# One projection per batch with its rounded halves stacked through DRAM, separate banks for the two score passes, and the value bias moved into the gelu

## The chip, the cores and the metric

The kernel runs on one core of a Trainium2 chip. The metric is the device time of one execution in microseconds (us). Every number of the profile comes from one profiled execution.

## The reference

Eight blocks follow each other on a residual x of 8 batches x 128 rows x 512 columns: four times an attention, then a feed-forward layer. The change touches the first attention alone:

```python
x = x + _L0_xattn_ref(_layernorm(x), ctx, mask, Wq, bq, Wk, bk, Wv, bv, Wo, bo)
# W = 128 (window), H = 8 heads, D = 128, DK = 64, dh = 8; patches are [d, 128] windows of a batch
q = einsum('ed,bdw->bew', Wq, qp) + bq[:, None]
k = einsum('ed,bdw->bew', Wk, qp) + bk[:, None]
val = einsum('ed,bdw->bew', Wv, vp) + bv[:, None]
scores = einsum('bhdi,bhdj->bhij', qh, kh) / sqrt(dh)
scores = where(mask > 0, scores, -1e9)
attn = softmax(scores)
o = gelu(einsum('bhij,bhdj->bhdi', attn, vh))
out = (einsum('de,bew->bdw', Wo, o) + bo[:, None]) * mask
```

## The kernel before

The order of every engine is written out by hand in `l0_attention`, and the engines meet only at semaphores. SP issues the DMAs of this stage.

The work is cut into 16 **units**: unit u is batch b = u // 2 and group g = u % 2 of four heads. The score products run in float32r, which keeps fewer bits than float32, so each head's eight rows of q and of k are split into a rounded part and a rest, and three products are stacked along the contraction: hi·hi, hi·lo, lo·hi. A head fills a slot of 32 partitions: three times eight rows, a row that carries the negated maximum (24) and a row for the mask (25). Before the change the stacking comes from the projection itself: `wq` and `wk` hold every head's weights three times, so that each unit needs two projections of 128x512 in float32 (`project`, L625 and L626), and selection columns (`C_SELQ`, `C_SELK`) pick the parts out on ScalarE and GpSimd.

A unit's steps, with the letters that the prediction uses:
- **P**: two projections into `K_BANK` and `Q_BANK`; ScalarE takes `q_lo` (L448) and `k_hi` (L456), VectorE makes `kf` (L514) and `q` (L521), GpSimd makes `k` (L432) and every batch's `key_mask` (L361, L364).
- **S**: plain scores, queries against keys, 16 matmuls for a unit in two halves (L655), each half into a pair of banks, `S_BANK + 2 * (s % 2)`.
- **M**: maximum over the keys on VectorE, one `tensor_reduce` for a half (L553).
- **T**: four transposes that turn the maxima (L664).
- **L**: `lower`, VectorE adds the turned maxima to `q` (L562).
- **K**: keyed scores, keys against queries, 16 matmuls (L672) in two halves, into the same pairs of banks as S.
- **E**: the exponential, one ScalarE activation for a half (L464).
- **V**: 16 float32 matmuls with the values (L683), which the trace shows as 32.
- **C**, **O**, **D**: ScalarE takes the sums out (L471), four transposes (L690), VectorE divides (L542, L544).
- **PV**: once per batch the values' projection (L633), which shares `K_BANK`; VectorE adds the bias bv (L531).

After the 16 units `turn_back`, a gelu, `project_out` and the residual follow for each of the 8 batches. Statistics of x (L100, L102) and `normalise` (L502) are VectorE's.

## Time and profile before

| | us |
|---|---|
| median of 3 runs | 1110.77 |
| lowest and highest | 1109.35, 1111.75 |
| span of the profiled execution, first to last instruction | 1113.1 |
| PE busy in the span | 956.4 (86%) |
| DVE, ACT, POOL busy | 710.9, 459.4, 368.4 |
| first attention: first keyed product to last division | 23.88 to 156.11 |

No time of the profiled execution beside its span is given; the span alone stands 2.3 us over the median of the runs. Busy time of PE is the union of its matmuls, which are pipelined and whose ends are modelled. In a timeline a row is a group of like instructions: start, duration, engine, line, operation, output and inputs, count, and in brackets the idle time of the engine before it with what ended it. PEclk is the granted TensorE clock, 1.00 for 2.4 GHz and 0.50 for 1.2 GHz; before 27 us it reads 1.00 although the matmuls there take as long as later ones at 0.50.

### The profile page before, as it was taken

To read this page: it belongs to the slowest core of one execution; us is meant where nothing else is said; L and a number is where in the kernel's file an instruction comes from. 1 tells how busy PE (TensorE), PEld (TensorE's weight loads), DVE (VectorE), ACT (ScalarE), POOL (GpSimd) and SP (SyncE) were. 2 spreads that over 40 slices of the span, in tenths; PEclk is the share of its full clock that TensorE was granted. 3 is DMA by queue.
4 is the path that set the end of the run, shared out by engine and by line. 5 is a ranking of instruction groups with operands and counts; after the bars stand their busy time and mean duration, and the time that the engine had idled before them with its cause. 6 is when DMAs were issued, how large, how long until landed. Compare 5 with 4: busy or idle time off the path is not lost. (4 is left out here: it accounts for less than half of the span.)

```text
span 1113.1 us, 14911 instructions
## 1 busy us (share of the span) xinstructions
PE 956.4 (86%) x4939; PEld 617.6 (55%) x4939; DVE 710.9 (64%) x1186; ACT 459.4 (41%) x672; POOL 368.4 (33%) x352
## 2 busy tenths in 40 slices
PE   5888884999999999999887688899987698779997
PEld 2555552655666666664454344444464465447886
DVE  5676547396778777874958853477745788445434
ACT  2454432324656566662225332344412465334130
POOL 5244203104757656752221320200010122038431
PEclk9899865899999999999987799699997899979999
DMA  8000102233978967655404100000003100022001
GB/s 315 1 2 1 57 2 90 87 133 129 335 278 306 348 240 262 221 190 199 160 1 180 39 0 1 20 2 1 1 1 132 67 1 0 1 94 77 24 15 39
DMA packets 32988, 112.69 MB, mean 101 GB/s; under 512 B 4304, under 2 KB 4624, under 8 KB 29840
## 3 DMA queue, kind: packets, MB, share of 16 engines
q1 hardware_dynamic: 25392, 87.08, 21.3%
q0 software_dynamic: 7520, 24.65, 6.4%
q8 instruction: 41, 0.67, 0.2%
q14 instruction: 35, 0.29, 0.1%
HBM read 132.69 MB, written 16.78 MB: 134 GB/s over the span
## 5 line engine op out<-in xcount | busy, mean ns | idle before, releaser
L1208 POOL DMA_INDIRECT f_picks<-f_turn_xn,f_target x47 | 114.1, 2428 | 75.1 <-ACT f_turn_xn L1097 74.5
L1624 PE MATMUL banks<-f_t_dn,f_z 128*128 128x512 f32 x188 | 88.5, 593 | 0.6 <-issue 0.6
L1352 DVE TENSOR_TENSOR f_gu_lo<-f_t_gu,f_gu_hi 128x2048 fp32r<-128x2048 f32 x24 | 55.0, 2293 | 14.2 <-ACT f_gu_hi L1083 11.5
L1352 DVE TENSOR_TENSOR f_xn_lo<-f_t_gu,f_xn_hi 128x2048 fp32r<-128x2048 f32 x23 | 52.7, 2292 | 16.4 <-ACT f_xn_hi L1083 16.4
L1202 POOL DMA_INDIRECT f_turn_xn<-f_xn_rows,f_token x47 | 47.4, 1008 | 43.0 <-DVE f_token L1346 18.7
L106 POOL TENSOR_TENSOR a_ahead_var_eps<-mean_var,eps 128x1 f32<-128x1 f32 x16 | 3.0, 190 | 162.5 <-DVE mean_var L102 162.5
L2315 ACT ACTIVATE a_e<-banks 128x1024 f32<-128x1024 f32 x32 | 32.8, 1024 | 53.3 <-PE banks L2414 53.2
L1090 ACT ACTIVATE f_sil<-banks 128x256 f32<-128x256 f32 x47 | 18.1, 384 | 79.3 <-PE banks L255 79.3
L164 PE MATMUL banks<-ident,f_turn_xn 128*128 128x128 f32 x96 | 22.0, 384 | 32.6 <-DVE f_turn_xn L172 32.6
L1083 ACT CAST f_gu_hi<-f_t_gu 128x2048 fp32r x24 | 45.7, 1905 | 9.5 <-DMA f_t_gu<-in_f_gu 7.2
L1083 ACT CAST f_xn_hi<-f_t_gu 128x2048 fp32r x23 | 43.7, 1901 | 12.9 <-DMA f_t_gu<-in_f_gu 10.5
L100 DVE BATCH_NORM_STATS2 stat<-x_res 128x6 f32<-128x512 f32 x64 | 44.3, 692 | 5.2 <-DMA x_res<-in_x 3.3
L464 ACT ACTIVATE a_e<-banks 128x1024 f32<-128x1024 f32 x32 | 31.0, 1021 | 36.6 <-PE banks L672 36.6
L432 POOL TENSOR_TENSOR a_k<-a_kf,a_k_sel 128x512 fp32r<-128x512 f32 x16 | 20.8, 1301 | 73.3 <-ACT a_k_sel L456 73.3
L1624 PEld LDWEIGHTS banks<-f_t_dn,f_z 128*128 128x128 f32 x188 | 32.1, 190 | 23.3 <-issue 23.2
L2352 DVE TENSOR_REDUCE a_mx<-banks 128x8 f32<-128x1024 f32 x32 | 39.1, 1222 | 8.5 <-PE banks L2396 8.5
L553 DVE TENSOR_REDUCE a_mx<-banks 128x8 f32<-128x1024 f32 x32 | 37.6, 1219 | 6.3 <-PE banks L655 6.3
L253 PE MATMUL banks<-f_gu_hi,f_xn_hi 128*128 128x512 f32 x96 | 40.0, 417 | 1.8 <-issue 1.7
L2428 PE MATMUL banks<-a_e,raw 128*32 128x512 f32 x128 | 35.4, 631 | 4.5 <-DVE a_ot_lo L2344 4.5
L106 POOL TENSOR_TENSOR f_ahead_var_eps<-mean_var,eps 128x1 f32<-128x1 f32 x24 | 9.0, 375 | 91.4 <-DVE mean_var L102 91.4
L253 PE MATMUL banks<-f_xn_hi 128*128 128x512 f32 x92 | 38.2, 415 | 1.1 <-issue 1.1
L3087 DVE TENSOR_TENSOR f_square<-f_relu 128x512 f32<-128x512 f32 x16 | 19.5, 1224 | 30.6 <-ACT f_relu L3030 25.6
(415 smaller groups left out, 2635.5 us busy)
## 6 DMA issues: line engine op xcount, KB each, us to landing
f_t_gu<-in_f_gu SPq DMA_DIRECT2D x47, 1024.0 KB
f_t_dn<-in_f_dn SPq DMA_DIRECT2D x47, 512.0 KB, 4.4
f_t_gu<-f_picks SPq DMA_DIRECT2D x8, 1024.0 KB, 5.1
f_xn_rows<-f_turn_xn SPq DMA_DIRECT2D x9, 256.0 KB, 2.6
x_res<-in_x SPq DMA_DIRECT2D x8, 256.0 KB, 6.9
a_ctx<-in_ctx SPq DMA_DIRECT2D x2, 1024.0 KB, 13.5
a_out_mask<-in_mask SPq DMA_DIRECT2D x1, 2048.0 KB, 15.8
a_ct<-in_ctx_turned SPq DMA_DIRECT2D x4, 512.0 KB, 7.9
```

Source lines behind the costliest of these rows:

```text
L100: dve.bn_stats(self.stat[:, b, :], src).then_inc(self.stat_ready, 1)
L253: pe.matmul(out, w_hi, m_hi, start=start, stop=False)
L464: act.activation(e[:, u % 2, 2 * (s % 2):2 * (s % 2) + 2, :], ps[:, s_banks(s), :], ACT.Exp, scale=scale).then_inc(exp_ready, 1)
L553: dve.tensor_reduce(mx[:, :, PAIR * (s % 2) + A0_MAX_ROW:PAIR * (s % 2 + 1):A0_SLOT].rearrange("p w r -> p r w"), ps[:, s_banks(s), :].rea ...
L1083: act.copy(t_gu_hi[t % 2], t_gu[:, bass.ds(i, 1), :, :].rearrange("p i c n -> p (i c n)"))\
L1202: pool.indirect_dma_start(t_rows[:, t % F0_BUFS, :], None, dram["f0_xn_rows"], bass.IndirectOffsetOnAxis(ap=token[:, t:t + 1], axis=0))\
L1208: pool.indirect_dma_start(dram["f0_picks_flat"], bass.IndirectOffsetOnAxis(ap=target[:, t:t + 1], axis=0), t_y[:, t % F0_BUFS, :], None).t ...
L1352: dve.tensor_tensor(t_gu_lo[t % 2], t_gu[:, bass.ds(i, 1), :, :].rearrange("p i c n -> p (i c n)"), t_gu_hi[t % 2].bitcast(F32), ALU.subtr ...
L1624: mm = pe.matmul(ps[:, TY_BANK + t % 2, :], t_zt[:, t % 2, c, :], t_dn[:, t % F0_BUFS, c, :], start=c == 0, stop=c == F0_IC - 1)
L2315: act.activation(e[:, u % 2, 2 * (s % 2):2 * (s % 2) + 2, :], ps[:, s_bank(s):s_bank(s) + 2, :], ACT.Exp, scale=scale).then_inc(exp_ready, 1)
L2352: dve.tensor_reduce(mx[:, tiles, A2_MAX_ROW:P:A2_SLOT].rearrange("p m r -> p r m"), ps[:, s_bank(s):s_bank(s) + 2, :].rearrange("p r (m j) ...
L2428: mm = pe.matmul(ps[A2_VSLOT * i:A2_VSLOT * (i + 1), O_BANK + u % 2, :], v[:, b // HB, b % HB, g * A2_PER_GROUP + i, :], e[:, u % 2, i, :] ...
```

## The change

- **One projection per batch.** q and k come out of one 128x512 projection (`wqk`, 64 rows of q above 64 of k). VectorE adds the bias and applies the mask (`keys_queries`), ScalarE rounds (`upper_part`), GpSimd subtracts (`lower_part`; for batch 0 VectorE).
- **Stacking by DMA.** SP writes the parts of a batch to a DRAM tensor `a0_parts` with five DMAs (`store`) and reads them back with four (`fetch`) into one of three buffers `a0_st`, 26 rows for each head. Constant rows and the mask row are written once, for all batches, by three more DMAs.
- **Three batches are projected ahead** (`A0_EARLY`); later ones follow in the odd units 1, 3, 5, 7 and 9.
- **Own banks.** S always writes banks 4 and 5, K always banks 6 and 7. A half of S therefore waits for the maximum of the half before, a half of K for the exponential before. PV has a bank of its own.
- **Loads.** Batches 3 to 7 of x are loaded after the fetches of batches 0, 1 and 2.
- **Moved to other engines.** `normalise` of batches 3 to 7 and one mask operation per batch are GpSimd's; the values are taken out by ScalarE without bias, and bv is the bias of the gelu.
- **Rows.** S and K contract over 26 rows instead of 32.

The core of the diff:

```diff
+                    def store(b):
+                        qs, ks = slice(0, A0_HEADS), slice(A0_HEADS, 2 * A0_HEADS)
+                        sp.wait_ge(qk_hi_ready, b + 1)
+                        hi, lo = qk_hi[:, b % 2, :].bitcast(F32), qk_lo[:, b % 2, :].bitcast(F32)
+                        sp.dma_start(part_of(b, slice(0, 2 * A0_HEADS), 0), hi).then_inc(parts_stored[b % 2], 16)
+                        sp.dma_start(part_of(b, qs, 1), hi[0:A0_DK]).then_inc(parts_stored[b % 2], 16)
+                        sp.dma_start(part_of(b, ks, 2), hi[A0_DK:P]).then_inc(parts_stored[b % 2], 16)
+                        sp.wait_ge(qk_lo_ready, b + 1)
+                        sp.dma_start(part_of(b, qs, 2), lo[0:A0_DK]).then_inc(parts_stored[b % 2], 16)
+                        sp.dma_start(part_of(b, ks, 1), lo[A0_DK:P]).then_inc(parts_stored[b % 2], 16)
+                    def fetch(b):
+                        sp.wait_ge(parts_stored[b % 2], 16 * A0_WRITES * (b // 2 + 1))
+                        if b < A0_BUFS:
+                            sp.wait_ge(st_zeroed, b + 1)
+                        else:
+                            sp.wait_ge(keyed_done, 2 * A0_GROUPS * (b - A0_BUFS + 1))
+                        for r in range(A0_PER_GROUP):
+                            sp.dma_start(st[r * A0_SLOT:r * A0_SLOT + A0_ROWS, b % A0_BUFS, :, :].bitcast(F32),
+                                         parts[b, r::A0_PER_GROUP].rearrange("j e n -> e j n")).then_inc(st_loaded[b % A0_BUFS][r // 2], 16)
...
+                    store(0)
+                    sp.wait_ge(fixed_stored, 16 * 3)
+                    fetch(0)
+                    load_x(3)
+                    store(1)
+                    fetch(1)
+                    load_x(4)
+                    load_x(5)
+                    store(2)
+                    fetch(2)
+                    load_x(6)
+                    load_x(7)
...
+                    kept(1)
+                    lower_part(1)
+                    clear(1)
+                    kept(2)
+                    lower_part(2)
+                    for i in range(2):
+                        pool.memset(v[:, i, :, :, :], 0.0).then_inc(zeroed, 1)
...
+                    clear(2)
+                    for b in range(3, B):
                         first.scale(pool, b)
+                        kept(b)
+                        normalise(b)
+                        lower_part(b)
...
+                    maximum(0)
+                    maximum(1)
+                    for b in range(A0_EARLY, B):
+                        statistics(b)
+                    for u in range(UNITS + 2):
+                        if u >= 2:
+                            divide(u - 2)
+                        if u + 1 < UNITS:
+                            maximum(2 * u + 2)
+                        if batch_at(u) is not None:
+                            keys_queries(batch_at(u))
                         if u < UNITS:
                             lower(u)
...
                         if u + 1 < UNITS:
                             maximum(2 * u + 3)
...
                     def scores(s):
...
+                        pe.wait_ge(st_loaded[b % A0_BUFS][s % 2], 16 * 2 * (b // A0_BUFS + 1))
+                        if s >= 1:
+                            pe.wait_ge(max_ready, s)
...
                     def keyed(s):
...
+                        if s >= 1:
+                            pe.wait_ge(exp_ready, s)
...
                     for u in range(UNITS + 1):
                         if u < UNITS:
-                            keyed(2 * u)
-                            keyed(2 * u + 1)
-                        if u == 0:
-                            project(2)
+                            turn_max(u)
+                        if u + 1 < UNITS:
+                            scores(2 * u + 2)
+                        if u >= 1:
+                            keyed(2 * u - 1)
+                        if batch_at(u) is not None:
+                            project(batch_at(u))
+                        if values_at(u) is not None:
+                            project_values(values_at(u))
                         if u >= 1:
                             values(u - 1)
...
                         if u + 1 < UNITS:
-                            scores(2 * u + 2)
                             scores(2 * u + 3)
+                        if u < UNITS:
+                            keyed(2 * u)
                         if u >= 1:
                             turn_outputs(u - 1)
-                        if u + 3 < UNITS:
-                            project(u + 3)
-                        if u + 1 < UNITS:
-                            turn_max(u + 1)
```

PE's order inside the loop. First before the change, an odd and an even unit (L672 is K, L683 V, L633 PV, L655 S, L690 O, L625 and L626 P, L664 T):

```order
L672 MATMUL banks<-a_q,a_k 128x128 x16
L683 MATMUL banks<-a_e,a_v 32x128 x16
L633 MATMUL banks<-raw,a_ctx 128x64 x4
L655 MATMUL banks<-a_k,a_q 128x128 x16
L690 MATMUL banks<-ident,a_osb 128x128 x4
L625 MATMUL banks<-a_xn,raw 128x512
L626 MATMUL banks<-a_xn,raw 128x512
L664 MATMUL banks<-ident,a_mx 128x128 x4
```

Then the change, from T of unit 3 to O of unit 2 (L735 is T, L726 S, L745 K, L697 P, L704 PV, L756 V, L763 O):

```order
L735 MATMUL banks<-ident,a_mx 128x128 x3
L726 MATMUL banks<-a_st 128x128 [waits a0_max_ready,a0_st_loaded_2_0]
L726 MATMUL banks<-a_st 128x128 x7
L745 MATMUL banks<-a_qm,a_st 128x128 [waits a0_exp_ready,a0_q_max_ready]
L745 MATMUL banks<-a_qm,a_st 128x128 x7
L697 MATMUL banks<-a_xn,raw 128x512 [waits a0_qk_ready,a0_xn_ready]
L704 MATMUL banks<-raw,a_ctx 128x64 [waits a0_v_ready,a0_ctx_loaded_1]
L704 MATMUL banks<-raw,a_ctx 128x64 x3
L756 MATMUL banks<-a_e,a_v 32x128 [waits a0_on_ready,a0_v_ready,a0_exp_ready]
L726 MATMUL banks<-a_st 128x128 [waits a0_max_ready,a0_st_loaded_2_1]
L745 MATMUL banks<-a_qm,a_st 128x128 [waits a0_exp_ready,a0_q_max_ready]
L763 MATMUL banks<-ident,a_osb 128x128 [waits a0_o_ready]
```

The two halves of S and of K no longer stand together: V and, in an odd unit, P and PV stand between them, and V waits for the second exponential of its own unit.

SP's queue in the change, from the write of batch 1 to the load of x for batches 6 and 7 (L418 to L423 are `store`, L432 is `fetch`, L394 `load_x`):

```order
L418 DMA a_parts<-a_qk_hi 16x8x512 [waits a0_qk_hi_ready]
L422 DMA a_parts<-a_qk_lo 8x8x512 [waits a0_qk_lo_ready]
L432 DMA a_st<-a_parts 26x4x512 [waits a0_st_zeroed,a0_parts_stored_1]
L432 DMA a_st<-a_parts 26x4x512 x3
L394 DMA x_res<-in_x 128x512 x2
L418 DMA a_parts<-a_qk_hi 16x8x512 [waits a0_qk_hi_ready]
L422 DMA a_parts<-a_qk_lo 8x8x512 [waits a0_qk_lo_ready]
L432 DMA a_st<-a_parts 26x4x512 [waits a0_st_zeroed,a0_parts_stored_0]
L432 DMA a_st<-a_parts 26x4x512 x3
L394 DMA x_res<-in_x 128x512 x2
```

Before, all eight loads of x were issued at the head of the queue with nothing that SP waited for between them; now the last two stand behind three waits for writes to land.

## Rows read from the trace of the kernel before

**Rows 1.** Windows: the loop, then two stretches of it at the low clock level

```profile
core 0: us, PE busy (x) PEld busy (x) DVE busy (x) ACT busy (x) POOL busy (x), PEclk, DMA share, GB/s
23.88:156.11 132.23, 110.81 (x1248) 75.78 (x1249) 79.65 (x122) 60.02 (x77) 42.04 (x33) 0.84 0.04 15
...
106.20:113.00 6.80, 6.31 (x20) 3.62 (x20) 3.77 (x7) 1.64 (x3) 1.27 (x1) 0.50 0.00 0
137.00:157.20 20.20, 15.40 (x169) 11.75 (x169) 5.29 (x10) 7.48 (x9) 0.00 (x0) 0.50 0.11 44
```

**Rows 2.** Timeline, an odd unit at the high level: start and duration first

```profile
67.19 0.69 PE L672 MATMUL banks<-a_q,a_k 32*128 32x128 f32 x16 [0.78 <-DVE a_q L562]
...
67.81 1.08 PE L683 MATMUL banks<-a_e,a_v 128*32 128x128 f32 x32
67.89 1.94 ACT L464 ACTIVATE a_e<-banks 128x1024 f32<-128x1024 f32 x2 [1.37 <-PE banks L672]
...
68.83 1.10 PE L633 MATMUL banks<-raw,a_ctx 128*128 128x64 f32 x8
...
69.86 0.78 PE L655 MATMUL banks<-a_k,a_q 32*128 32x128 f32 x16
...
70.56 2.36 DVE L553 TENSOR_REDUCE a_mx<-banks 128x8 f32<-128x1024 f32 x2 [0.17 <-PE banks L655]
...
71.06 1.02 PE L625 MATMUL banks<-a_xn,raw 128*128 128x512 f32 x2
...
71.92 1.02 PE L626 MATMUL banks<-a_xn,raw 128*128 128x512 f32 x2
...
72.97 0.42 PEld L664 LDWEIGHTS banks<-ident,a_mx 128*128 128x128 f32 x4 [0.86 <-DVE a_mx L553]
```

**Rows 3.** The page's costliest groups: the exponential of one half (E)

```profile
L464 ACT ACTIVATE a_e<-banks 128x1024 f32<-128x1024 f32 x32 | 31.0, 1021 | 36.6 <-PE banks L672 36.6
```

**Rows 4.** Timeline at the low level, and the loop's last division

```profile
125.26 1.91 PE L625 MATMUL banks<-a_xn,raw 128*128 128x512 f32 x2
...
126.96 1.92 PE L626 MATMUL banks<-a_xn,raw 128*128 128x512 f32 x2
...
137.74 1.14 PE L672 MATMUL banks<-a_q,a_k 32*128 32x128 f32 x16 [0.78 <-DVE a_q L562]
...
138.81 1.93 PE L683 MATMUL banks<-a_e,a_v 128*32 128x128 f32 x32
...
140.68 1.41 PE L655 MATMUL banks<-a_k,a_q 32*128 32x128 f32 x16
...
141.83 2.36 DVE L553 TENSOR_REDUCE a_mx<-banks 128x8 f32<-128x1024 f32 x2 [4.15 <-PE banks L655]
...
144.24 0.72 PEld L664 LDWEIGHTS banks<-ident,a_mx 128*128 128x128 f32 x4 [1.51 <-DVE a_mx L553]
...
155.82 0.29 DVE L544 TENSOR_TENSOR a_on_all<-banks,a_rec 128x128 f32<-128x128 f32 x1
```

**Rows 5.** Waits of the first 150 us: total, times and longest

```profile
PE banks L672 <- DVE a_q L562: 12.5, 16, 0.8
```

**Rows 6.** Timeline of the start of the kernel

```profile
0.95 1.84 POOL L405 MEMSET a_v<- 128x1024 f32 x2
1.20 0.42 SPq L378 DMA_DIRECT2D raw<-in_a_first  x1
...
5.83 2.05 PE L625 MATMUL banks<-a_xn,raw 128*128 128x512 f32 x2 [5.83 <-DVE a_xn L502]
...
12.33 1.26 POOL L432 TENSOR_TENSOR a_k<-a_kf,a_k_sel 128x512 fp32r<-128x512 f32 x1 [0.49 <-ACT a_k_sel L456]
...
19.19 2.01 POOL L361 TENSOR_SCALAR raw<-raw,a_cols 128x512 f32<-128x512 f32 x1
...
23.88 1.15 PE L672 MATMUL banks<-a_q,a_k 32*128 32x128 f32 x16 [0.78 <-DVE a_q L562]
```

**Rows 7.** Tile f_xn_rows: landing of nine writes of 256 KB to DRAM

```profile
DMA to landing us min/median/max: 2.0/3.9/9.2
```

More of the change, by code:

```diff
@@ new lines, in load_x, with load_ctx, load_mask @@
+                    def load_x(b):
+                        sp.dma_start(core.x[:, b, :], dram["x"][b]).then_inc(x_loaded[b], 16)
+                    def load_ctx(i):
+                        sp.dma_start(ctx[:, 2 * i:2 * i + 2, :], dram["ctx"][2 * i:2 * i + 2].rearrange("b p s -> p b s"))\
+                          .then_inc(ctx_loaded[i], 16)
+                    def load_mask(i, first, last):
+                        out = late_mask[:, :, :] if first >= HB else core.raw[:, 1, first * D:last * D]
+                        src = dram["mask"][first:last]
+                        if first < HB:
+                            src = src.rearrange("b s -> (b s)")
+                        sp.dma_start(out, src.partition_broadcast(P)).then_inc(mask_loaded[i], 16)
@@ new lines, in part_of, with same @@
+                    def part_of(b, jobs, part):
+                        return parts[b, jobs, part * A0_DH:(part + 1) * A0_DH, :]
+                    def same(row):
+                        return row.unsqueeze(1).broadcast_to([B, A0_HEADS, row.shape[1]])
+                    def store(b):
[8 more added lines that the diff above has]
+                        sp.dma_start(part_of(b, ks, 1), lo[A0_DK:P]).then_inc(parts_stored[b % 2], 16)
@@ L393, in _ @@
                       .then_inc(out_mask_loaded, 16)
-                    sp.wait_ge(proj_done, UNITS)
-                    sp.wait_ge(v_ready, B)
-                    sp.wait_ge(kf_ready, UNITS)
+                    for b in range(4, B):
+                        store(b)
+                        fetch(b)
+                    sp.wait_ge(proj_done, B)
+                    sp.wait_ge(qk_ready, B)
+                    sp.wait_ge(v_done, B)
                     core.prefetch(sp, "a0")
@@ L403, in _, with clear, lower_part, kept @@
                     pool.memset(core.ident[:, :], 0.0).then_inc(const_ready, 1)
-                    for i in range(2):
-                        pool.memset(v[:, i, :, :, :], 0.0)
-                    pool.memset(mx[:, :, :], 0.0).then_inc(zeroed, 1)
+                    def clear(i):
+                        pool.memset(st[:, i, :, :].bitcast(F32), 0.0).then_inc(st_zeroed, 1)
+                    def lower_part(b):
+                        pool.wait_ge(qk_hi_ready, b + 1)
+                        pool.wait_ge(qk_lo_ready, b)
+                        pool.tensor_tensor(qk_lo[:, b % 2, :], qk[:, b % 2, :], qk_hi[:, b % 2, :].bitcast(F32),
+                                           ALU.subtract).then_inc(qk_lo_ready, 1)
+                    def kept(b):
+                        pool.wait_ge(mask_loaded[1 if b < HB else 2], 16)
+                        keep(pool, b).then_inc(keep_ready, 1)
+                    def normalise(b):
+                        pool.wait_ge(first.rstd_ready, b + 1)
+                        pool.wait_ge(proj_done, b - 1)
+                        pool.tensor_scalar(xn[:, b % 2, :], core.x[:, b, :], core.mean(b),
+                                           core.rstd(b), ALU.subtract, ALU.mult).then_inc(xn_ready, 1)
                     pool.wait_ge(const_ready, 3)
@@ new lines, in _ @@
+                    pool.memset(mx[:, :, :], 0.0).then_inc(mx_zeroed, 1)
+                    for b in range(1, 3):
+                        first.scale(pool, b)
+                    pool.wait_ge(cols_ready, 1)
+                    kept(1)
[5 more added lines that the diff above has]
+                        pool.memset(v[:, i, :, :, :], 0.0).then_inc(zeroed, 1)
+                    pool.wait_ge(zeroed, 2)
@@ L670, in keyed @@
                         pe.wait_ge(q_max_ready, u + 1)
[L671 to L673 removed]
+                        if s >= 1:
+                            pe.wait_ge(exp_ready, s)
+                        for rows, r, w, win in heads(pair(s), A0_ROWS):
+                            mm = pe.matmul(ps[:, E_BANK + r % 2, win], k_of(u, rows, win),
+                                           qm[rows, u % 2, win], start=True, stop=True)
                         mm.then_inc(keyed_done, 1)
```

362 lines of the change are left out of this document (151 added, 211 removed).

## Prediction

> **What bounds the kernel now.** I read the windows view first. The first attention's loop runs from the first keyed product at 23.88 [rows 6] to the last division, which ends at 156.11 [rows 4], so 132.2 us for 16 units, 8.3 each. In it TensorE is busy 110.8 us and its granted clock is 0.84 on average [rows 1]. With two levels, 1.00 (2.4 GHz) and 0.50 (1.2 GHz), 0.84 means 32% of the loop at the low one. The timeline of an odd unit then shows why a unit at the high level lasts some 7.2 us: K, V, PV, S, O, P and T follow each other with hardly a hole, and only the maximum (2.36 us on VectorE beside P) and the lowering leave PE waiting [rows 2]. PE is the bound, and the clock sets its pace. The last thing to see is what level PE has when it has less to do: from 137.0 to 157.2 no projection runs, PE is busy 15.4 of 20.2 us, and the clock reads 0.50 throughout, whereas from 106.2 to 113.0, also at 0.50, PE is busy 6.3 of 6.8 us, and that stretch ends after 6.8 us [rows 1]. Nothing outside this stage is touched, so the rest of the kernel is taken as it is.
>
> **Term 1, the loop at the high level.** A unit loses two projections of 0.86 us each (71.06 to 71.92) [rows 2] and gets half of one back. What remains cannot simply be added up, since each half of S now waits for the maximum before it and each half of K for the exponential before it. The ring of waits is: T, half of S, half of K, E, V, the other half of S, M, and T again. By rows: T 0.42; half of S 0.31 (K takes 0.62 from 67.19 to 67.81 for both halves, and S is of its kind); K to E 0.70 (67.19 to 67.89); E 1.02 [rows 3] and 0.14 to hand over, my estimate; V 1.02 (67.81 to 68.83); S to M 0.70 (69.86 to 70.56); M 1.21, half of 2.36 and the start [rows 2]. That is **5.5 us**. In an odd unit P 0.86 and PV 1.03 (68.83 to 69.86) stand between K and V. They fit into K to E and E (1.86 us) but for some 0.3 us, so 5.8 to 5.9. VectorE (two maxima, lower, division, half of a `keys_queries`: some 4.2 us) and ScalarE (two exponentials, C, half of a cast and of a copy: some 3.1) have slack. Fifteen steps of 5.6 to 5.9 and 6.7 for the last unit's tail make **92 us** for the whole loop.
>
> **Term 2, the loop at the low level.** The same ring: T 0.85 (the weights of T alone take 0.72), half of S 0.54 (K: 137.74 to 138.81 for two), K to E 1.15, as S to M from 140.68 to 141.83, E 1.16, V 1.87 (138.81 to 140.68), S to M 1.15, M 1.27 [rows 4]: **8.0 us**. In an odd unit P is 1.70 (125.26 to 126.96) [rows 4] and PV some 1.8 (an estimate, 1.03 at the high level times the 1.8 of V), which sticks out by 1.7: 9.7. Five odd units carry both, so all 16 units take **137 us**.
>
> **Term 3, which level.** At the high level an even unit of the change has 3.1 us of matmuls in 5.6 (T, O, two halves of S and K, V), 56%; before, its even unit had 4.9 of 7.2, 67%, and yet a third of the loop stood at the low level [rows 1]. So it will fall sooner. At the low level the change fills 5.9 of 8.0 and 9.4 of 9.7 us, 81% on average, between the 76% that never rose and the 93% that did [rows 1]. I expect a level that goes up and down all the time, and take 55% at the low one, against 32% before. Then the loop is 1 / (0.45/92 + 0.55/137) = **112 us**, or 20 less than now. The bounds are both levels alone: 92 and 137.
>
> The Trainium skill (TensorE: Matmul & The Clock Gate, "Why this matters for your kernels") has another rule: only gaps of PE of more than some 3 us put the clock down. The longest wait of K for the lowering, the hole in each unit, is 0.8 us [rows 5], and a third of the loop stood at the low level all the same [rows 1], so the trace disagrees; by that rule the loop would take 92.
>
> **Term 4, the start.** The first keyed product stands at 23.88 [rows 6]. In the change it needs `lower(0)`, and VectorE reaches that only after the statistics of all eight batches; batches 6 and 7 of x are loaded behind the third fetch. So SP's queue sets it, where each instruction waits for the one before. One issue takes 0.47 us (0.42 and the step to the next [rows 6]). The first projection starts at 5.8 and takes 2 us [rows 6]; bias, mask and rounding make `qk_hi` ready at 9.2. Then three times: five writes 2.35, landing 2.3, four reads 1.9, and x. No row has such a write; the nearest are the nine writes of 256 KB to DRAM, which land after 2.0 to 9.2 us, 3.9 in the median [rows 7]. I take 2.3, near the lowest, because the bytes are few and little else is in flight by then. The walk: writes 9.3 to 11.8, landed 14.0; fetch to 16.0, x of batch 3; second writes 16.5 to 18.8, landed 21.1; fetch to 23.1, two loads of x to 24.0; third writes to 26.4, landed 28.7; fetch to 30.6; x of 6 and 7 issued by 31.5, landed at 34; statistics, a maximum 1.2 and the lowering 0.7 follow. First keyed product at **36.8**, 12.9 later than now.
>
> GpSimd runs beside this and must not be later: mask operations of 2.0 us, subtractions of 1.3, and the clearing of three buffers at 1.9 each (twice 128x1024 takes 1.84) [rows 6] put `clear(2)` at 27, before 28.7; so it costs nothing, and with landings at 2.0 it would be next. PE, waiting for the start, costs nothing else.
>
> A rule of the Trainium skill speaks against these writes (DMA: Bandwidth & Descriptors, "Rules for kernel authors"): a transfer whose outermost dimension is 8 runs on at most 8 of the 16 engines, and four of the five writes have 8 heads outermost. By it a write of 128 KB costs its engines what one of 256 KB does, and the three rounds would be some 4 us longer, 1107 instead of 1103.5. No row of this kernel shows such a write.
>
> **Moved at no cost.** Writes and reads of batches 3 to 7 start three batches ahead of their use, 6 units or some 40 us, against a round of 8: hidden; if they were late, each would cost its round. GpSimd's `normalise` and mask, some 4 us a batch against 14, are hidden likewise. PV's own bank and the copy on ScalarE lie in its slack. The bias in the gelu adds no instruction; VectorE bounds that part. 26 rows instead of 32 stream the same columns: nothing. The final prefetch stays under the loop's tail.
>
> **The sum.** +12.9 - 20 = **-7.3 us**. The profiled span of 1113.1 would become 1105.8. It stands 2.3 over the median of the runs, 1110.8, from which I forecast **1103.5**.
>
> **Rivals.**
> - *All low.* After the slow start PE never gets its high level, as in the 20.2 us at 0.50 [rows 1]. The loop takes 137, 5 more than now, and with the start +18: **1129**, slower. For it: little projecting is left, and in the stretch that ended at 113 it was projections that kept PE full. Against it: an odd unit has PE full for over 9 us. It decides from a low share of 75%, where loop gain and late start cancel out.
> - *Slow landings.* Writes land after 3.9 and more, as in the median of [rows 7], and x after them: each of three rounds is 1.6 longer, the x behind the last too, +7: **1110.5**, no change; at 6 us it is 1117. For it: eight engines; against it: small transfers.
> - *All high.* The clock stays up, as the skill's rule has it: loop 92, 20 less than my value: **1083**. Against it stands the third of the loop at 0.50 with more work for PE than the change leaves.
>
> **Chances.** My forecast 0.53, all low 0.13, slow landings 0.20, all high 0.10, and 0.04 for something that I don't see. 0.2%, or 2.2 us, is about what a measurement of this kernel can tell from no change. The forecast's own spread is 1093 to 1114 (start 34 to 40, low share 0.4 to 0.7), of which a part lies within 0.2% or above. Faster: 0.42 of it, all high 0.10, and 0.06 of slow landings, 0.58. Same: 0.06 and 0.06, 0.12. Slower: 0.05, all low 0.13, 0.08 and 0.04, 0.30. The range that holds it 8 times in 10 leaves out most of all low and of all high: **1088 to 1124**.
>
> **What would show it.** Right if: first keyed product of the loop at 34 to 40, with VectorE's statistics waiting for the DMA of x before it; high units of 5.5 to 5.9 us and low ones of 8 to 9.7; a PEclk near 0.72 over the loop; E waiting for K and V for E in each unit. Term 4 is wrong if the product comes after 44; term 3 if PEclk is over 0.85 or under 0.60; terms 1 and 2 if a unit at a known level is off by over 0.7 us. Writes of later batches that show as waits of S would overturn the part on what is hidden.

## The result, and the profile after

The changed kernel is slower: 1137.82 us in the median of 4 runs (1131.82, 1143.82, 1143.86 and 1124.33) beside 1111.26 for the kernel before on the same chip, a ratio of 1.0133 with a 95% interval of [1.0090, 1.0175]. The ratio leaves out the two slow runs near 1144, which stand over 1.5% above the fastest, so it rests on two runs, and the median does not leave them out. The profiled execution took 1131.82 us with a span of 1130.0, 16.9 over the span of before. That divides into three stretches: the first keyed product comes at 55.33 instead of 23.88 (+31.4), the loop takes 121.3 instead of 132.2 us (-11.0), and the rest 953.4 instead of 957.0 (-3.6). Forecast were +12.9, -20 and 0.

The page of the changed kernel: the span, then the exponential [rows 3], the statistics, and the writes [rows 7].

```profile
span 1130.0 us, 14829 instructions
...
L561 ACT ACTIVATE a_e<-banks 128x1024 f32<-128x1024 f32 x32 | 32.8, 1024 | 64.1 <-PE banks L745 63.7
L100 DVE BATCH_NORM_STATS2 stat<-x_res 128x6 f32<-128x512 f32 x64 | 44.3, 693 | 21.7 <-DMA x_res<-in_x 19.8
...
f_xn_rows<-f_turn_xn SPq DMA_DIRECT2D x9, 256.0 KB, 2.0
```

E costs what it did. New is the 19.8 us that VectorE's statistics wait for x. The rows that gave my bounds for a write, the nine of [rows 7], have a median of 2.0 us here by both views, and before 2.6 on the page and 3.9 by the tile's view in [rows 7], so they were a weak price.

**The start**, by the timeline of SP and then of VectorE:

```profile
4.14 3.05 SPq L405 DMA_DIRECT2D raw<-in_mask  x1
7.24 4.20 SPq L397 DMA_DIRECT2D a_ctx<-in_ctx  x1
...
11.90 0.64 SPq L418 DMA_DIRECT2D a_parts<-a_qk_hi  x1
...
13.27 1.85 SPq L420 DMA_DIRECT2D a_parts<-a_qk_hi  x1
15.17 1.97 SPq L422 DMA_DIRECT2D a_parts<-a_qk_lo  x1
17.18 0.77 SPq L423 DMA_DIRECT2D a_parts<-a_qk_lo  x1
21.43 1.59 SPq L432 DMA_DIRECT2D a_st<-a_parts  x4
...
32.08 1.57 SPq L432 DMA_DIRECT2D a_st<-a_parts  x4
...
37.03 0.57 SPq L423 DMA_DIRECT2D a_parts<-a_qk_lo  x1
43.31 1.60 SPq L432 DMA_DIRECT2D a_st<-a_parts  x4
44.95 0.84 SPq L394 DMA_DIRECT2D x_res<-in_x  x2
```

```profile
17.88 0.75 DVE L612 SCALAR_TENSOR_TENSOR a_qk<-banks,a_cols,raw 128x512 f32<-128x512 f32 x1 [6.03 <-POOL raw L366]
...
51.85 0.69 DVE L100 BATCH_NORM_STATS2 stat<-x_res 128x6 f32<-128x512 f32 x1 [10.00 <-DMA x_res<-in_x]
...
54.60 0.68 DVE L642 TENSOR_TENSOR a_qm<-banks,a_st 128x512 fp32r<-128x512 f32 x1
```

The shape is the one forecast: write, land, fetch, three times, then x of 6 and 7, the statistics, and only then the lowering. The sizes are not. An issue of a DMA mostly takes 0.3 to 0.6 us here, but those of the mask and ctx take 3.05 and 4.20 and two of the writes 1.85 and 1.97. The third round's writes end their issue at 37.60 and the fetch follows at 43.31, 5.7 later. The five issues themselves, one behind the other, take 6.05 us in the first round (11.90 to 17.95) and 3.5 and 3.0 in the others.

**The loop**, by windows: its stretches at one clock level each, then the whole [rows 1].

```profile
core 0: us, PE busy (x) PEld busy (x) DVE busy (x) ACT busy (x) POOL busy (x), PEclk, DMA share, GB/s
55.33:82.10 26.77, 24.26 (x226) 18.27 (x228) 11.56 (x15) 9.30 (x12) 7.48 (x7) 1.00 0.61 180
82.10:109.40 27.30, 21.03 (x360) 15.65 (x352) 17.69 (x26) 14.53 (x19) 14.78 (x14) 1.00 0.56 143
109.40:153.80 44.40, 40.26 (x420) 31.03 (x420) 19.40 (x28) 15.34 (x20) 3.27 (x2) 0.50 0.26 67
153.80:157.20 3.40, 2.60 (x44) 1.91 (x40) 1.83 (x4) 1.67 (x3) 0.00 (x0) 1.00 0.93 386
157.20:176.60 19.40, 15.01 (x156) 11.64 (x157) 5.14 (x10) 8.11 (x9) 0.00 (x0) 0.50 0.02 8
55.33:176.60 121.27, 103.15 (x1192) 78.49 (x1191) 55.62 (x81) 48.93 (x61) 25.53 (x21) 0.74 0.39 108
```

Here the granted clock misleads. It reads 1.00 from 55.33 to 82.10, but a maximum's turn (T) lasts 1.12 us there, as at 0.50, against 0.66 at the high level. The column shows no drop, presumably because it has no change on record before the first rise (not shown). By durations, each stretch taken whole at the level of its turns, 26.8 + 44.4 + 19.4 = 90.6 us of 121.3 are at the low level, **75%**. Timeline of PE, VectorE and ScalarE, an odd unit at the high level [rows 2], then one at the low level [rows 4]:

```profile
89.80 0.66 PE L735 MATMUL banks<-ident,a_mx 128*128 128x128 f32 x4 [0.55 <-DVE a_mx L632]
...
91.00 1.12 PE L697 MATMUL banks<-a_xn,raw 128*128 128x512 f32 x2
91.09 1.23 DVE L632 TENSOR_REDUCE a_mx<-banks 128x8 f32<-128x1024 f32 x1 [0.86 <-PE banks L726]
91.18 1.02 ACT L561 ACTIVATE a_e<-banks 128x1024 f32<-128x1024 f32 x1 [1.55 <-PE banks L745]
...
91.96 1.00 PE L704 MATMUL banks<-raw,a_ctx 128*128 128x64 f32 x8
...
92.89 1.08 PE L756 MATMUL banks<-a_e,a_v 128*32 128x128 f32 x32
...
94.61 1.23 DVE L632 TENSOR_REDUCE a_mx<-banks 128x8 f32<-128x1024 f32 x1 [1.04 <-PE banks L726]
...
95.89 0.65 PE L735 MATMUL banks<-ident,a_mx 128*128 128x128 f32 x4 [0.55 <-DVE a_mx L632]
```

```profile
131.90 1.12 PE L735 MATMUL banks<-ident,a_mx 128*128 128x128 f32 x4 [0.26 <-DVE a_mx L632]
...
134.01 1.97 PE L704 MATMUL banks<-raw,a_ctx 128*128 128x64 f32 x8
...
135.91 1.94 PE L756 MATMUL banks<-a_e,a_v 128*32 128x128 f32 x32
...
138.94 1.23 DVE L632 TENSOR_REDUCE a_mx<-banks 128x8 f32<-128x1024 f32 x1 [3.01 <-PE banks L726]
```

From T to T an odd unit takes 6.09 us here and an even one 5.45; at the low level 10.02 with a projection, 8.32 with the values' projection alone (131.90 to 140.22) and 7.68 without either. No unit of a known level is off my rings by more than 0.35. A half of S and a half of K, which I had put one behind the other, run beside each other: in unit 4 they start at 84.93 and 84.96 us. The waits of PE in the loop (total, times, longest) no longer have K waiting for the lowering [rows 5]; the first row is the ring's new one, V for the exponential, in 9 of the 16 units, and the second is T for the maximum:

```profile
PE banks L756 <- ACT a_e L561: 10.5, 9, 1.2
...
PE banks L735 <- DVE a_mx L632: 6.2, 15, 0.8
```

**The rest.** The gelu with its bias takes 0.68 us instead of 0.59. The same stretch behind the loop, first after and then before, shows that nothing comes of it:

```profile
176.60:220.00 43.40, 26.00 (x87) 12.39 (x85) 30.10 (x50) 12.00 (x18) 10.84 (x18) 0.66 0.25 89
```

```profile
156.10:199.50 43.40, 25.98 (x87) 12.37 (x86) 30.16 (x50) 11.27 (x18) 10.80 (x18) 0.66 0.25 89
```

The 3.6 us of the whole rest are no effect of the edit that I can name: in profiled executions of the experiments below, which leave it as it is, it takes 950.9 to 963.6 us.

### The profile page after: what moved, and what is told of

Same layout as the page of the kernel before. It is cut to its first block and busy times, and to the rows that moved or that the text cites. A ratio compares the mean times of both kernels' runs of the same rounds, so it can differ in the third digit from the quotient of the medians.

```text
span 1130.0 us, 14829 instructions
## 1 busy us (share of the span) xinstructions
PE 946.1 (84%) x4891; PEld 619.6 (55%) x4891; DVE 691.1 (61%) x1151; ACT 448.0 (40%) x656; POOL 366.0 (32%) x346
## 5 line engine op out<-in xcount | busy, mean ns | idle before, releaser
L100 DVE BATCH_NORM_STATS2 stat<-x_res 128x6 f32<-128x512 f32 x64 | 44.3, 693 | 21.7 <-DMA x_res<-in_x 19.8
L726 PE MATMUL banks<-a_st 26*128 26x128 f32 x256 | 30.2, 372 | 26.3 <-DVE a_mx L632 23.0
L726 PEld LDWEIGHTS banks<-a_st 26*128 26x128 f32 x256 | 24.8, 268 | 35.2 <-issue 33.6
L255 PE MATMUL banks<-f_gu_hi,f_xn_lo 128*128 128x512 f32 x96 | 38.6, 403 | 0.0
```

Of the source, the lines that this page charges most:

```text
L100: dve.bn_stats(self.stat[:, b, :], src).then_inc(self.stat_ready, 1)
L255: return pe.matmul(out, w_lo, m_hi, start=False, stop=stop)
L726: mm = pe.matmul(ps[:, S_BANK + r % 2, win], q_of(u, rows, win), k_of(u, rows, win), start=True, stop=True)
```

## Experiments

Two losses were to be told apart: a late start, and a clock that is low for longer than before. "K0" is the first keyed product and "end" the end of the loop's last division, each in the one profiled execution. A "turn" is a T, one for each of the 16 units; it lasts 1.02 us or more at the low level and 0.60 to 0.66 at the high one. The times of one kernel on one chip spread by up to 1.7%, so for the whole only the ratios to the kernel before are compared, with their intervals in brackets (the change has 1.0133 [1.0090, 1.0175]). An interval of a percent cannot tell a gain of 10 us from none.

**e1_x_early.** The change's loads of x of 3 to 7, moved up:

```
 load_x(1)
-load_x(2)
+for b in range(2, B):
+    load_x(b)
```

> The change, with the loads of x of batches 3 to 7 issued right behind that of batch 2, ahead of everything that waits. Theory A (in the changed kernel VectorE's statistics of batches 3 to 7 wait 19.8 us for x, whose loads stand behind the fetches, and the first lowering stands behind them): the waits of the statistics for x go, the first keyed product comes at 36 to 40 instead of 55.3 us, and the whole is 14 to 18 us faster than the change, about 0.998 of the kernel before. Five issues more ahead of the first writes cost some 2.5 us, which is in that. Rival B (the three rounds of write and fetch hold the loop by themselves): the first keyed product stays over 50 us and the gain is under 4 us.

Measured: K0 41.1, end 171.9, loop 130.7; ratio to before 1.0170 [1.0084, 1.0255]. The waits for x are gone and K0 is 14.2 earlier, one us off the forecast of A, but the end moves by only 4.7 and the whole by nothing that shows; the 14 to 18 us of A are missed. The loop is 9.4 longer: 13 of its 16 turns last 1.11 or 1.12 us, after the change 10. In this execution two thirds of the early start were given back at the low level.

**e2_stats_late.**

```
-for b in range(A0_EARLY, B):
-    statistics(b)
 for u in range(UNITS + 2):
     ...
         maximum(2 * u + 3)
+    if u + A0_EARLY < B:
+        statistics(u + A0_EARLY)
```

> The change, with VectorE's statistics of batches 3 to 7 taken from ahead of the loop into its units 0 to 4, behind the second maximum of each; no load is moved. Theory A: the first lowering needs only batch 0's fetch and the maxima, so the first keyed product comes at 30 to 33 us, 22 to 25 earlier; some 3 us of it are given back where a unit waits for batch 1's fetch or a statistic for x of batches 4 and 5. The whole is 18 to 24 us faster than the change, about 0.994 of the kernel before. Rival B (rounds hold the loop): unit 2 waits for batch 1's fetch and unit 4 for batch 2's so long that the loop's end moves by under 6 us.

Measured: K0 34.9, end 160.3, loop 125.4; 1.0120 [1.0034, 1.0207]. The end is 16.3 earlier, so the rounds do not hold the loop and B falls, though S waits once for a fetch, for 3.2 us. The early start reaches the end with 10 of 16 turns low, as many as after the change. The rest took 963.6, and of the 18 to 24 us nothing beyond the spread shows in the whole; the two intervals would leave room for some 15. Unit 1 takes 13.7 instead of 10.0 us, since PE waits 3.6 for GpSimd's normalised x of batch 3.

**e4_both**, the two edits together.

> The two edits together: loads of x of batches 3 to 7 early, and their statistics in units 0 to 4 of the loop. Theory A: the first keyed product comes at 32 to 36 us (two to three later than with the statistics moved alone, for the five issues ahead of the first writes), no statistic waits for x, and the whole is 18 to 23 us faster than the change, within 0.2% of the run with the statistics moved alone. Rival B as there: under 6 us.

Measured: K0 40.4, end 162.2; 1.0142 [1.0070, 1.0215]. The end is 14.4 earlier than after the change, but the whole shows none of it. K0 is 5.5 later than with the statistics moved alone, not 2 to 3: with five more loads queued, the first write's issue alone takes 4.25 us, from 9.80.

**e3_filler.** One more matmul (identity by ctx, into the projection's bank) where a unit has no projection:

```
 if batch_at(u) is not None:
     project(batch_at(u))
+elif u < UNITS:
+    again(min(A0_EARLY + u // 2, B))
```

> The change, with one more 128x128x512 matmul in each unit that has no projection, into the projection's bank, between the keyed product and the values; its result is not read. It gives PE back work that the change took away. Theory C (the clock is low in 75% of the loop because PE has holes, and units at the low level are 2 us longer): the granted clock of the loop rises from 0.63 to over 0.8 and the loop takes 95 to 108 us instead of 121, though PE has more to do; the whole is 13 to 25 us faster. Rival D (the level does not hang on this work): the clock stays near 0.63, the extra matmul of 0.86 or 1.70 us hides behind the exponential or costs up to 12 times 1.7, and the loop takes 121 to 135 us.

Measured: K0 55.3, end 155.2, loop **99.9**; ratio **0.9992** [0.9960, 1.0023]. Windows of its loop (columns as above, here and below): the first stretch, the last, and the whole.

```profile
55.30:66.50 11.20, 9.97 (x96) 7.40 (x95) 4.86 (x5) 4.59 (x6) 3.47 (x4) 1.00 0.16 47
...
136.50:155.20 18.70, 14.85 (x232) 10.46 (x221) 6.96 (x13) 9.95 (x12) 0.00 (x0) 0.95 0.23 86
55.30:155.20 99.90, 86.75 (x1212) 61.16 (x1212) 55.52 (x81) 48.84 (x61) 25.52 (x21) 0.96 0.45 132
```

Eleven matmuls more make the loop 21.4 us shorter, with the start untouched. (The 0.63 in the expectation counts the stretch before the first rise as low; the column reads 0.74 there and 0.96 here.) Two of its 16 turns are low, instead of 10. Units at the high level keep their 5.45 and 6.09, so the matmul hides behind the exponential; two odd units take 7.70, since the level falls and comes back inside them (PEclk 0.50 from 86 to 88 us). The whole is 1.4% faster than the change by the ratios, and the intervals do not meet. C stands, D falls.

One profiled execution could be luck, but the count holds over all of them. Without the extra matmul the change and its variants (e1, e2, e4, e6, e7, e13) have 8 to 14 low turns of 16; with it (e3, e5, e8, e9, e10, e11, e14) they have 0 to 3. The mean granted clock of the whole execution is 0.932 to 0.940 in all ten runs of e3 and 0.898 to 0.924 in the four of the change. What in PE's work sets the level stays open.

**e12_before_filler.** The same remedy for the kernel before, two matmuls in each of three units:

```
 if u + 3 < UNITS:
     project(u + 3)
+elif u < UNITS:
+    again()
```

> The kernel before the change, with two extra matmuls in each of units 13 to 15, where it has no projections; nobody reads them. There the granted clock is 0.50 from 137 to 157 us. Theory C holds for the kernel before too: the last stretch stays at the high level, units 14 and 15 and the tail are 3 to 6 us shorter together, and the loop's end comes at 150 to 153 instead of 156.1; 0.996 of the kernel before. The two stretches at 106 and 123 us stay, since those units have their projections. Rival D: the level does not hang on this; the end comes at 156 to 160.

Measured: end 150.0, ratio 0.9968 [0.9930, 1.0006]. Windows, from 137 us to the end of the loop, beside 0.50 from 137.0 to 157.2 in [rows 1]:

```profile
137.00:150.00 13.00, 9.79 (x121) 6.59 (x120) 4.55 (x9) 4.92 (x7) 0.00 (x0) 1.00 0.00 1
```

The end is 6.1 earlier, so the effect is not one of the change alone; the gain in the whole cannot be told from none.

**e5_late_filler**, the statistics in the loop and the extra matmul.

> Two edits to the change that were run apart: the statistics of batches 3 to 7 in the loop's units 0 to 4, and the extra matmul in the units without a projection. Theory A with C (late start and low clock are two separate losses): first keyed product at 35 as with the first edit, units of 5.5 and 6.1 us from about 60 us on, the loop's end at 137 to 143 instead of 155.2 (extra matmul alone), and the whole 10 to 18 us faster than that run, about 0.988 of the kernel before. Rival E (an earlier start only meets the rounds of writes and fetches, so that the loop's second and third batch wait for them): the end comes at 148 or later and the gain is under 7 us.

Measured: K0 35.7, end 141.2; ratio **0.9884** [0.9806, 0.9963], by the ratios 12 us below e3, with intervals that just meet (0.9963 and 0.9960). K0 is 19.6 earlier than in e3 and the end 14.0. That is Theory A with C, and E falls, though S waits for a fetch three times in the loop, 7.3 us in all.

**e6_three_writes.**

```
-sp.dma_start(part_of(b, qs, 1), hi[0:A0_DK])
-sp.dma_start(part_of(b, ks, 2), hi[A0_DK:P])
+sp.dma_start(part_of(b, slice(0, 2 * A0_HEADS), 1), hi)
 ...
-sp.dma_start(part_of(b, qs, 2), lo[0:A0_DK])
-sp.dma_start(part_of(b, ks, 1), lo[A0_DK:P])
+sp.dma_start(part_of(b, slice(0, 2 * A0_HEADS), 2), lo)
```

> The change, with each batch written by three DMAs of 16 heads (256 KB each) instead of one of 16 and four of 8 heads (128 KB each): the same bytes into the same rows. The second and third part of the keys come out exchanged, so the scores' small correction terms are others; nothing else changes. In the changed kernel the fetch of a batch in the loop is issued 6.4 to 6.7 us after the first write's issue, and the DMA share stands at 0.44 to 0.46 when only 8-head writes are under way (123 to 125 us). Theory F (a write of 8 heads runs on at most 8 engines, so its bytes take twice the time): 4.3 to 5.0 us instead of 6.4 to 6.7, with a DMA share over 0.8 until the end. Rival G (only the number of issues counts, two fewer at 0.62 each, and the share of 0.45 is a limit of writing): 5.2 to 5.5 us, with the share still near 0.45 after the last issue. The whole is 4 to 7 us faster than the change by F, 2 to 4 by G, through the three rounds ahead of the loop.

The keys' second part holds hi here, so the scores count hi by hi twice: more than a correction term. Windows while such writes are under way, of this kernel and then of the change with only 8-head writes left:

```profile
110.50:113.00 2.50, 2.50 (x39) 1.97 (x32) 0.49 (x1) 0.99 (x2) 2.42 (x4) 0.50 0.96 293
```

```profile
123.00:125.00 2.00, 1.74 (x8) 1.28 (x8) 1.61 (x3) 1.02 (x1) 0.00 (x0) 0.50 0.45 135
```

The DMA share is 0.96 instead of 0.45, and a batch's last bytes move 4.0 us after its first issue instead of 5.7. The interval that both theories were to be told apart by, from first write to fetch inside the loop, does not do so: it is 5.3 to 6.7 us, but a fetch there also waits for a half of K, which ends last each time. By the share F is right about engines: 8 heads outermost keep half of the 16 busy. It is wrong about worth. Ahead of the loop, rounds two and three need 7.3 and 7.7 us from first write to fetch instead of 8.6 and 8.7, which is the two issues less, as G had it: after the last issue the writes land no sooner (5.5 and 5.9 us for 5.1 and 5.7). K0 comes at 51.4. The whole is no faster, 1.0246 [1.0150, 1.0342]: 14 of its 16 turns are low and its loop takes 133.8 us.

**e13_thin_fetch.**

```
+rows = 2 if b < A0_BUFS else A0_ROWS
-    parts[b, r::A0_PER_GROUP].rearrange("j e n -> e j n")
+    parts[b, r::A0_PER_GROUP, 0:rows].rearrange("j e n -> e j n")
```

> The change, with the fetches of batches 0 to 2 reading 2 of their 26 rows (64 KB a batch instead of 832); the other rows stay zero, so the scores of these batches are not the right ones. Theory L (ahead of the loop the second and third batch's writes share the DMA engines with the fetch issued just before them and with x): the time from the last issue of the writes to the next fetch falls from 5.1 and 5.7 us to 2.7 to 4.0 in rounds two and three, the DMA share between them falls well under 0.9, and the first keyed product comes 4 to 8 us earlier, at 47 to 51. Rival M (writes to DRAM take that long at this place by themselves, or x holds them): 4.8 us or more in both rounds and a first keyed product over 52.

Measured: K0 48.0, end 168.4; 1.0101 [1.0038, 1.0163]. SP's timeline, end of the second and third writes and the fetches behind them:

```profile
26.16 0.57 SPq L423 DMA_DIRECT2D a_parts<-a_qk_lo  x1
30.28 1.14 SPq L433 DMA_DIRECT2D a_st<-a_parts  x4
...
34.93 0.93 SPq L423 DMA_DIRECT2D a_parts<-a_qk_lo  x1
39.86 1.17 SPq L433 DMA_DIRECT2D a_st<-a_parts  x4
```

Landing takes 3.55 and 4.0 us instead of 5.1 and 5.7, and the first keyed product is 7.3 earlier: L. A round's writes land 1.6 and 1.7 us later behind a fetch of 832 KB than behind one of 64. That is about half of what I had missed; the rest of it, up from my 2.3, no run explains. With little else under way, in the loop, they land 2.7 to 3.1 us after the last issue.

**e7_light_start.** On e2: the first mask load shortened to batch 1, the rest and ctx behind the first fetch, PV of batch 0 behind the scores.

> The change with the statistics moved into the loop, and in addition a lighter start: ahead of the first writes stands the mask of batch 1 alone (256 KB instead of 768 KB for three batches) and no ctx; ctx of batches 0 and 1 and the mask of batches 2 and 3 are loaded behind the first fetch, and the values' projection of batch 0 stands behind the scores. Theory H (the start is late because 1.3 MB of loads stand in the DMA queue ahead of the first writes, which stalls SP's issues by some 6 us, and because VectorE waits for the mask of batch 1): the second bias and mask operation comes at 13 to 15 us instead of 17.6, the first fetch at 16 to 18 instead of 21.0, and the first keyed product at 29 to 32 instead of 34.9. Rival I (GpSimd's own chain of mask, subtraction and clearing paces the start): the second bias and mask operation stays over 16.5, and the first keyed product over 33.5. The whole moves with the first keyed product, less what the clock gives or takes.

Measured: second bias and mask operation 16.1, first fetch 20.1, K0 **41.4**, end 172.5; 1.0125 [1.0033, 1.0217]. It tests neither theory at its end, because the edit made a wait of its own: VectorE needs batch 2's mask ahead of the first maximum, that mask now stood behind the fetch, and its third bias and mask operation came at 32.6. Of the start it shows 1.5 us won for batch 1 and 0.9 for the first fetch.

**e8_all_three**, e7 with the extra matmul.

> The three edits together: statistics in the loop, extra matmul in the units without a projection, lighter start. If all three losses are separate: first keyed product at 29 to 32 us, the loop's end at 132 to 138, the whole 3 to 6 us faster than the run with two of them, about 0.984 of the kernel before. If an earlier start meets the rounds of the next batches: no faster than that run.

Measured: K0 41.4, end 145.5; 0.9926 [0.9892, 0.9959]. Not faster than e5: K0 is 5.7 later than there, for e7's reason.

**e9_start2.** On e5: x and statistics of batch 3 early, ctx of 0 and 1 behind the first fetch, masks in place.

> The run with statistics in the loop and the extra matmul (first keyed product 35.7, loop's end 141.2 us), with two more edits: x of batch 3 is loaded behind x of batch 2 and its statistics stand ahead of the first maximum, and ctx of batches 0 and 1 is loaded behind the first fetch (the masks stay where they are), the values' projection of batch 0 behind the scores. There unit 1 took 13.7 us, of which PE waits 3.6 for the normalised x of batch 3. Theory: unit 1 falls to 10 or 11 us, the first keyed product comes at 32 to 35, the loop's end at 134 to 138, and the whole is 3 to 7 us faster than that run. Rival: batch 3's normalisation is late through GpSimd's own chain of masks and clearings; unit 1 stays over 13 and the end over 138.5.

Measured: K0 35.7, end 144.6; 0.9909 [0.9866, 0.9952]. Unit 1 falls to 10.0 as expected, but unit 3 grows from 7.7 to 13.3, where PE waits 4.6 us for the normalised x of batch 4, behind a mask that lands at 55.3. The wait moved on by two units, K0 did not move, and the end and the whole came out no better than e5 (expected: 134 to 138).

**e10_warm.** On e9, `warm(n)` being n times four 128x128 matmuls of the identity by itself (the expectation calls them transposes):

```
+warm(5)
 scores(0)
+warm(2)
 scores(1)
 project_values(0)
+warm(1)
```

> The run beside it, with 32 more transposes of the identity matrix on PE while it waits at the start: 20 ahead of the first scores, 8 between the two halves and 4 behind, some 8 us of work that nobody reads. In all runs so far the matmuls of the first two to four units last as long as at the low level. Theory C carried to the start: PE busy from 24 us on has its high level by unit 1, units 0 to 2 are each 2 to 4 us shorter, and the loop's end comes 5 to 9 us earlier than in the run beside it: 127 to 131, the whole about 0.978 of the kernel before. Rival: the extra work only pushes the first scores back by 2 to 4 us, or the waits of unit 1 drop the level again: end within 2 us of the run beside it, or later.

Measured: end 138.9, 5.7 earlier; 0.9894 [0.9837, 0.9951]. Timeline, the first turn of unit 0 (1.06 us long in e9, at 31.67), and PE's waits from 54 to 66 us:

```profile
38.72 0.60 PE L747 MATMUL banks<-ident,a_mx 128*128 128x128 f32 x4
```

```profile
PE banks L698 <- POOL a_xn L500: 2.9, 1, 2.9
```

Both answers hold at once. Every turn from the first is at the high level (4.6, 6.1, 5.5 us where e9 has 6.5, 10.0, 5.5), and the extra work pushes the first turn back by 7 us. The end at 127 to 131 was expected without that and without unit 3's wait; the whole cannot be told from e9. Unit 3 still takes 10.65, with the wait shown.

**e14_best.** On e10: 8, 4 and 4 such matmuls, and batch 4's mask alone behind the second fetch.

> All edits that helped, tuned: statistics in the loop (batch 3's ahead of it), the extra matmul in units without a projection, ctx of batches 0 and 1 behind the first fetch, 16 instead of 32 extra transposes at the start (8 ahead of the first scores, 4 between the halves, 4 behind), and the mask of batch 4 alone loaded behind the second fetch, those of 5 to 7 where the late mask was. If the late mask is what made unit 3 wait: unit 3 takes 6 to 9 us instead of 10.7, T of unit 0 starts at 32 to 36, the loop's end comes at 132 to 137 (138.9 with 32 transposes, 144.6 with none), and the whole is at 0.984 to 0.989 of the kernel before. If not: unit 3 stays over 10 and the end over 137.5.

Measured: unit 3 takes 6.09, so the mask was its cause. T of unit 0 stands at 37.0 and lasts 1.02 us, so 8 matmuls ahead of the first scores did not bring the high level that 20 brought. Both T and the end miss the expectation (32 to 36, 132 to 137). The profiled execution was the slowest of six (1107.65) and ends its loop at 144.3, with unit 1 and the stretch from 82 to 96 us at the low level. The median is 1099.92, the ratio **0.9852** [0.9815, 0.9889]. Its interval overlaps e5's; both are faster than the kernel before.

**e11_alternate_banks.** On e3, scores and keyed scores of half s both in pair s mod 2:

```
-ps[:, S_BANK + r % 2, win]    (scores)      -ps[:, E_BANK + r % 2, win]    (keyed)
+ps[:, S_BANK + r, win]                      +ps[:, S_BANK + r, win]
-scores: wait max_ready >= s                 +scores: wait exp_ready >= s - 3
-keyed:  wait exp_ready >= s                 +keyed:  wait max_ready >= min(s + 3, 32)
```

> The change with the extra matmul (units of 5.45 and 6.09 us at the high level), with the change's own bank pairs undone: half s of plain and of keyed scores both go to pair s mod 2, as before the change, in the change's order of instructions. The waits that this needs (a half of plain scores for the exponential four halves before, a keyed half for the maximum of the half that it overwrites) are all met by then in this order. Theory J (what shortened the unit is the order and the lost projections, not which banks are used): even units 5.3 to 5.6 and odd 6.0 to 6.2 at the high level. Rival K (the own pairs let both kinds of scores run at the same time, which alternating pairs forbid): 5.9 and 6.6 or more.

Measured, in its only execution: 5.45 and 6.09 at the high level, end 155.2 as e3, and a half of S still starts beside a half of K (81.57 and 81.60 us). J: in this order, own bank pairs by themselves bring nothing. The order and the lost projections are what is left; they were not run apart.

## Why the prediction was wrong

I said 1103.5 and faster; it is slower by 1.3% and outside the range of 1088 to 1124. The profiled span adds up: 1105.8 + 18.5 (start) + 9.3 (loop) - 3.6 (rest) = 1130.0.

- **Terms 1 and 2, right.** High units 5.45 and 6.09 against 5.5 to 5.6 and 5.8 to 5.9; low ones 7.68 and 10.02 against 8.0 and 9.7. The waits of the ring are there (T for the maximum 15 times, V for E 9 times), and e11 shows that the length does not hang on the banks. The sum was closer than its parts: T to S takes 0.58 for 0.42, and S and K beside each other take 0.3 less than one behind the other.
- **Term 3, mis-sized: the step "take 55% at the low one".** It was 75%. With that the same formula gives 1 / (0.25/92 + 0.75/137) = 122 us, and 121.3 was measured. The sign that I named for it came true by luck: PEclk near 0.72 was expected and 0.74 is read, only because 26.8 us at the low level read 1.00. That less work for PE lowers the clock was right, and e3 shows it by putting work back. The way from busy shares to 55% was not: I reckoned with PE busy for 81% of the time at the low level, and from 109.4 to 153.8 it was busy for 40.3 of 44.4 us, 91%, and stayed low, while before the change 93% stood in a stretch that ended after 6.8 us. The error was to choose a middle value with no row for it, and to count no cost for a PE that enters the loop slow. Two of the rivals came together: the low share reached the 75% that "all low" named, and landings were slow besides. By my own numbers gain and late start cancel already at 70%, where the loop takes 119.3.
- **What the two losses do to each other, not settled.** In profiled executions the start and the end move earlier by, against the change: e1 14.2 and 4.7, e2 20.5 and 16.3, e4 14.9 and 14.4, e7 13.9 and 4.1, e13 7.3 and 8.2; against e3, with the extra matmul: e5 19.6 and 14.0, e8 13.9 and 9.7. So without the matmul anything from a third to the whole of an early start reaches the end, as the low turns (8 to 13) fall, and with it about 70%. In the whole only e5 shows the gain, and by intervals that just meet.
- **Term 4, mis-sized: K0 at 55.3 for 36.8.** By steps: the first fetch at 21.4 for 14.0 (first write 2.6 late behind the mask's and ctx's issues, the five issues 6.05 us instead of 2.35, landing 1.2 longer); rounds of 10.65 and 11.2 for 7.1 and 7.6; x of 6 and 7 landed 6.1 us after its issue for 2.5. The step that failed is "little else is in flight by then", which gave 2.3 us for a landing where 3.5, 5.1 and 5.7 were measured: the fetch of the batch before is in flight, as e13 shows for 1.6 us a round, and ahead of the first write 1.3 MB of masks and ctx. That issues stall, I had not costed at all; my 0.47 came from the second issue of the kernel, with one load ahead of it.
- **GpSimd beside it, partly wrong.** `clear(2)` ended at 31, not 27, and VectorE waited 6.03 us for the mask operation of batch 1. In the unchanged start this hid behind the rounds; e2 and e9 show PE waiting for GpSimd's normalised x as the next wait (3.6 of the 13.7 us of unit 1, then 4.6 of the 13.3 of unit 3, there behind a late mask).
- **Moved at no cost, right.** Fetches of batches 3 to 7 never held S in the loop; the gelu's 0.09 us are hidden.
- **The Trainium skill's two rules.** Of TensorE: Matmul & The Clock Gate, "Why this matters for your kernels": the row there asks for no gaps of over some 3 us between bursts of matmuls; it does not say, as I had put it, that only such gaps lower the clock. Read my way, the trace disagrees again, with the clock at 0.50 for 44.4 us in which PE's longest wait was 1.2. Of DMA: Bandwidth & Descriptors, "Rules for kernel authors": the trace agrees on the engines (share 0.45 against 0.96), but e6 puts the worth of following the rule, ahead of the loop, at no more than the issues saved.
- **What a measurement can tell.** I had put it at 0.2%. The interval of the result is 0.4% to either side, and those of the experiments 0.3% to 1.0%.

## What to carry over

When an edit takes work from the engine that bounds a stage and that engine's clock is seen at two levels, cost the stage at both, and ask first what keeps the clock up; here eleven matmuls that nobody reads were worth 21 us of a 121 us loop. Judge a shortened start by the end of the stage and not by its first instruction: between a third and the whole of it arrived here, and in each execution the clock fell at other places of the loop behind it. Price a DMA by what is in its queues at that moment, issues too, and after each wait that is removed look for the one behind it.

## What was not expected of the hardware

- The granted clock in the profile read 1.00 from 55.3 to 82.1 us, where T took 1.12 us, the duration of the low level; ahead of the first rise only durations tell.
- An issue on SP that elsewhere takes 0.3 to 0.6 us took 3.05 and 4.20 in the change, and 1.85 and 1.97 for two writes behind 1.3 MB of masks and ctx; with five more loads of x ahead (e1) the first write took 4.63.
- With 20 matmuls of 128x128 ahead of the first scores and 8 between its halves PE had the high level in unit 0 (T 0.60 us, e10), where e9 without them has T at 1.06 and 1.12 us in units 0 and 1, and e14 with 8 and 4 has 1.02 and 1.12.
- Halves of S and of K, which work on other rows of partitions, start 0.03 us apart in the loop although the program has them one behind the other.
- The stages behind the loop, the same in the change and its variants, took 950.9 to 963.6 us, and the two levels came at other places in them.
